# Local attention's routing and row projections move from the mixing piece into the global attention piece; all key sums first, values last

## The chip, the cores and the metric

The kernel runs on one core of one Trainium2 chip. What counts is the device time of one execution in microseconds (us), over all eight images. The engines are TensorE (PE, with its weight loads as PEld), VectorE (DVE), ScalarE (ACT), GpSimd (Pool) and SyncE (SP, which issues most DMAs).

## The reference, cut to what matters

Eight images of 128 channels and 32x32 points go through a local attention block with a convolutional tail, then a global attention block, then a mixture of experts.

```
# local attention ("a"): windows of 2x2 points, 256 windows, 4 selected by 8 heads x 16 channels
q, kv = rows(x) @ wq, rows(x) @ wkv            # per point
logit = mean(q) @ mean(k).T ; idx = top_k(logit, 4)      # routing
k_sel, v_sel = kv[idx]                          # 4 windows x 4 points = 16 keys
out = softmax(q . k_sel) . v_sel + dwconv5x5(v) # "lepe": 25 taps
x = x + out
x = x + fc2(relu(dwconv3x3(fc1(x))))
# global attention ("c"): 1024 tokens, 4 heads x 32 channels, distance mask
t = t + softmax(q k^T * mask) v @ Wo            # of layernorm(t)
# experts: 8, the best 2 of each token
t = t + sum_e combine[:, e] * (gelu(t' @ w1[e]) @ w2[e])   # t' = layernorm(t)
```

## The kernel before, in words

Each engine has its own program, written out by hand and held together by counting semaphores. Each runs its queue strictly in order. The loop over images is software-pipelined over three images: in turn n the kernel runs the global attention and the experts of image n, the convolution block and the q, k, v of image n+1 (`second`), and the local attention's front of image n+2 (`first`). A turn has two pieces, `attention` and `mixing`.

**Attention.** 32 units u (8 blocks of 128 queries by 4 heads). For each, PE computes 128x1024 scores (`("scores", u)`), DVE multiplies them by the distance band and finds the maximum (`scale_scores`, L1069), ACT takes the exponential (L734), PE transposes the result (`("turned", u)`, L540), ACT copies it out (L742), and PE multiplies it by the values one block later (`times_values`, L591). `projected` adds the output projection `wo` to the residual in two halves. Between units, at those in `WINDOW_STEPS_AT`, DVE runs one step each of the local attention of image n+1: tile 1's softmax and its value steps.

**Mixing.** PE follows `mixing_order()`: layer norm of image n (`centred`, `var`, `rstd`), router, the 3x3 convolution of image n+1 as matmuls with diagonal weights (`("dw", ...)`, L505), `start` and `combine` of the experts' result, then for eight experts `hidden` (L557, gelu on ACT) and `expert` (L560), which DVE adds up in `accumulate` (L1179, eight instructions per expert). Beside the experts come `fc2` of image n+1 (L514), its layer norm, and its q, k and v, which DVE finishes in `values` and `low(h)` (L1166).

**Local attention of image n+2.** `first_half` on DVE: `sums` of the four points of a window (L895), `choose` (max and index of the logits, L918 and L922), and eight `rows(t, p)`, each of which adds the bias to one projection of 128 windows (L905 for q, L906 for k and v). SP stores KV to a table in DRAM when all are done (`store_table`); Pool gathers the four chosen windows into KVSEL (`gathers`, L1299), multiplies keys by queries in 8 halves per tile (`key_product`, L1312), and DVE sums the products over channels (`sum_products`, L952). Each product lies in one of two halves of KV, so `key_product` i waits until sum i-2 is done. Then come per tile the softmax steps (`less_maximum` L962 and L963, ACT's `a_exp`, `sum_keys` L968) and four pairs of value steps (`multiply_values` L976, `attend` L983). After the last key sum Pool runs the 25 `taps` of the 5x5 convolution, each a product (L1325) and a sum into XLEPE (L1328). `window_residual` adds the attended rows to XLEPE in the next turn (L1021) and raises `x1_ready`, for which `fc1` waits.

In `second_half` the steps run in this order: key sums of tile 0, its softmax, its value steps woven with the key sums of tile 1, tile 1's softmax, its values. The first 26 (`EARLY_STEPS`) run in mixing between the experts' accumulations, the last ten in attention.

**PSUM.** Ring A has two banks of 512 columns (`psA`), ring B three of 1024 (`psB`). An entry's bank is its place in the emission order modulo the number of banks, and PE waits until the entry before it on that bank has been read out (`b_free`). Routing, rows and the values of the image use ring A; ring B has 115 entries in a turn, so the ring's last entry, k of head 3, and the first of the next turn, `("scores", 1)`, share a bank.

Where the routing stood in mixing:

```
PROJECTIONS_AFTER = {("centred", 1, 1): [(0, 0), (0, 1)], ("fc1", 0): [(0, 2), (0, 3)], ("var", 1, 1): [(1, 0), (1, 1)],
                     ("fc1", 1): [(1, 2)], ("rstd", 1, 1): [(1, 3)]}
```

Of the kernel before, what the change touches and what calls it, by code (L numbers as in the profile page):

```python
# [79 lines left out]
class Ring:  # L80

    def __init__(self, entries, slots):
        self.place, self.uses = {}, [0] * slots
        for i, name in enumerate(entries):
            s = i % slots
            self.place[name] = (s, self.uses[s])
            self.uses[s] += 1

    def slot(self, name):
        return self.place[name][0]

    def turn(self, name, n):
        s, k = self.place[name]
        return n * self.uses[s] + k + 1


class SharedRing(Ring):

    def __init__(self, first, middle, second, slots):
        super().__init__(first + middle + second, slots)
        self.first, self.middle = first, middle

    def turn(self, name, m):

        s, k = self.place[name]  # L110
        if name in self.middle:
            m = m + 1
        turn = m * self.uses[s] + k + 1
        if not (isinstance(m, int) and m == 0 and name in self.first):
            turn = turn - sum(self.place[other][0] == s for other in self.middle)
        if isinstance(m, int) and m == IMAGES:
            turn -= sum(self.place[other][0] == s for other in self.first)
        return turn


RING_A = SharedRing(["windows", "logits"] + [("qkv", t, p) for t in range(WTILES) for p in range(PX)] + [("v", 0), ("v", 1)],
                    [("pv", t) for t in range(TT)], [("attended", t) for t in range(WTILES)], 2)


class EarlyRing(Ring):

    def __init__(self, entries, early, slots):
        super().__init__(entries, slots)  # L130
        self.entries, self.early = entries, early

    def turn(self, name, n):
        s, k = self.place[name]
        on_slot = [other for other in self.early if self.place[other][0] == s]
        if name in self.early:
            if isinstance(n, int) and n == 0:
                return on_slot.index(name) + 1
            n = n - 1
# [1306 lines left out]
```

## Time and profile before

| what | value |
|---|---|
| median of 3 runs | 2264.81 us (2260.95 to 2265.35) |
| the profiled execution: its own time / its span | 2260.87 us / 2259.3 us |
| mean granted TensorE clock | 0.853 |
| busy: PE, DVE, Pool, ACT | 71%, 65%, 50%, 41% of the span |
| chain that ended last | PE 40%, DVE 23%, issue 16%, ACT 6%, Pool 5% |
| DVE waits for PE's expert results (L1179 for L560) | 310.6 us in all |
| Pool waits for the table store before its gathers | 250.0 us in all |

Times are from the start of the span. "Busy" is the time in which instructions of an engine run; the granted clock is the share of full speed (2.4 GHz) that PE was given. In a timeline a row gives start, duration, engine, line, operation, output and inputs, and the number of equal instructions merged into it; in brackets stands the idle time of the engine just before it, and what ended that. Rows below come from one turn of the loop, 849 to 1120 us, and a few from the start.

### The profile page before, as it was taken

The numbers are of one execution on the slowest core, as the hardware profiler recorded it, in microseconds if no ns is written. First come the engines' busy times: TensorE is split into PE (matmuls) and PEld (weight loads), VectorE is DVE, ScalarE is ACT, GpSimd is POOL, SyncE is SP. The second block draws the span as 40 slices with busy tenths as digits, with TensorE's granted clock in tenths as the row PEclk, the third lists the DMA queues.
The fourth block names the chain that finished last, engine by engine and source line by source line (L and its number), as shares of the span: only waits on it lengthen the run. The fifth ranks groups of instructions, "written<-read, shape, count | busy, mean of one in ns | idle before, by whom it ended". The sixth has DMA issues, their size and how long they took to land.

```text
span 2259.3 us, 39866 instructions
## 1 busy us (share of the span) xinstructions
PE 1611.4 (71%) x15168; PEld 1058.7 (47%) x15168; DVE 1471.6 (65%) x2564; ACT 933.5 (41%) x1285; POOL 1121.6 (50%) x582
## 2 busy tenths in 40 slices
PE   2004658895689857887578966788667875789897
PEld 1002325553455535555355544555355553555565
DVE  3893488638883498726886288854888268951654
ACT  0001237432563226633374234634256332754682
POOL 0994549433692329724495346934288233950000
PEclk9557878998799878988798987999779897989999
DMA  4201100030001100030000300011000200000000
GB/s 128 74 0 66 48 0 2 5 109 0 11 1 67 48 10 1 2 104 10 10 1 1 105 9 11 1 62 52 10 1 1 94 10 10 1 1 1 10 2 10
DMA packets 26138, 61.75 MB, mean 27 GB/s; under 512 B 4192, under 2 KB 13408, under 8 KB 25824
## 3 DMA queue, kind: packets, MB, share of 16 engines
q0 software_dynamic: 9216, 33.56, 4.3%
q1 hardware_dynamic: 16736, 25.60, 3.5%
q8 instruction: 131, 2.15, 0.4%
q14 instruction: 55, 0.45, 0.1%
HBM read 46.56 MB, written 12.58 MB: 26 GB/s over the span
## 4 chain that ended last, share of the span: by engine, by line
PE 40%; DVE 23%; issue 16%; ACT 6%; POOL 5%; DVEq 1%; ACTq 0%; POOLq 0%
PE psB L505 7%; PE psB L560 6%; DVE Q L983 6%; PE psB L540 5%; PE psB L408 5%; DVE P L1069 4%; DVE PT L1179 3%; PE psB L557 3%; POOL XLEPE L1328 3%; PE psB L514 3%; DVE STACKED L1166 2%; PE psA L591 2%; DVE KVSEL L952 2%; PE psA L423 2%; POOL KV L1325 2%
## 5 line engine op out<-in xcount | busy, mean ns | idle before, releaser
L1328 POOL TENSOR_TENSOR XLEPE<-XLEPE,KV 128x1024 f32<-128x1024 f32 x200 | 509.6, 2548 | 16.7
L1312 POOL TENSOR_TENSOR KV<-KVSEL,Q 128x1024 f32<-128x1024 f32 x112 | 267.4, 2406 | 444.9 <-DVE KVSEL L952 229.9
L540 PE MATMUL psB<-W,P 128*128 128x128 f32 x2048 | 319.6, 305 | 107.7 <-DVE NEGMAX L1069 100.7
L1069 DVE CUSTOM_DVE_ANT_0 P<-psB,W 128x1024 f32<-128x1024 f32 x256 | 312.3, 1220 | 99.8 <-PE psB L408 56.8
L734 ACT ACTIVATE P<-P,NEGMAX 128x1024 f32<-128x1024 f32 x256 | 293.0, 1145 | 186.4 <-DVE NEGMAX L1072 184.4
L1325 POOL TENSOR_SCALAR KV<-V_PAD,W 128x1024 f32<-128x1024 f32 x200 | 280.3, 1402 | 138.3 <-DVE KVSEL L952 98.3
L540 PEld LDWEIGHTS psB<-W,P 128*128 128x128 f32 x2048 | 257.4, 156 | 184.9 <-DVE NEGMAX L1069 96.4
L1179 DVE SCALAR_TENSOR_TENSOR PT<-psB,PT 128x128 f32<-128x128 f32 x512 | 138.2, 343 | 313.8 <-PE psB L560 310.6
L742 ACT ACTIVATE PT<-psB 128x1024 f32<-128x1024 f32 x256 | 260.7, 1018 | 59.4 <-PE psB L540 56.5
L408 PE MATMUL psB<-STACKED 96*128 96x512 f32 x512 | 205.9, 490 | 78.8 <-DVEq L1169 60.5
L560 PE MATMUL psB<-W,P 128*128 128x128 f32 x1024 | 159.6, 321 | 128.1 <-DVEq L1169 44.4
L983 DVE TENSOR_REDUCE Q<-PROD 128x128 f32<-128x2048 f32 x64 | 239.3, 3738 | 0.3
L560 PEld LDWEIGHTS psB<-W,P 128*128 128x128 f32 x1024 | 149.6, 231 | 160.5 <-issue 66.0
L1299 POOL DMA_INDIRECT KVSEL<-window_table,CHOSEN x64 | 60.9, 952 | 290.1 <-DMA window_table<-KV 250.0
L505 PE MATMUL psB<-H_PAD,DIAG 32*32 32x512 f32 x4608 | 167.9, 631 | 16.9 <-ACTq L687 14.8
L408 PE MATMUL psB<-TN,W 128*96 128x512 f32 x256 | 142.3, 707 | 45.8 <-DVEq L1169 45.8
L591 PE MATMUL psA<-PT,V 128*32 128x128 f32 x4096 | 170.2, 291 | 3.3 <-issue 2.2
L746 ACT ACTIVATE P<-psB,W 128x1024 f32<-128x1024 f32 x64 | 71.1, 1111 | 222.7 <-PE psB L557 222.7
L753 ACT ACTIVATE STACKED<-psB,W 96x1024 fp32r<-96x1024 f32 x64 | 70.2, 1108 | 207.4 <-PE psB L408 207.4
L591 PEld LDWEIGHTS psA<-PT,V 128*32 128x32 f32 x4096 | 103.6, 114 | 89.3 <-issue 88.5
L505 PEld LDWEIGHTS psB<-H_PAD,DIAG 32*32 32x32 f32 x4608 | 101.2, 105 | 84.1 <-issue 56.0
L408 PEld LDWEIGHTS psB<-STACKED 96*128 96x128 f32 x512 | 90.9, 218 | 93.8 <-DVEq L1169 65.6
(126 smaller groups left out, 2131.8 us busy)
## 6 DMA issues: line engine op xcount, KB each, us to landing
window_table<-KV SPq DMA_DIRECT2D x8, 1024.0 KB, 4.4
X<-x_by_window_dram SPq DMA_DIRECT2D x8, 512.0 KB
XLEPE<-x_dram SPq DMA_DIRECT2D x8, 512.0 KB, 3.5
out_dram<-PT SPq DMA_DIRECT2D x8, 512.0 KB, 3.4
W<-packed_dram SPq DMA_DIRECT2D x1, 3714.5 KB, 11.6
KVSEL<-window_table,CHOSEN POOLq DMA_INDIRECT x64, 5.4
FC<-packed_dram SPq DMA_DIRECT2D x8, 64.0 KB, 2.3
PROD<-gains_dram SPq DMA_DIRECT2D x1, 256.0 KB, 12.0
```

Of the source, the lines that this page charges most:

```text
L408: mm = pe.matmul(ps[:, h * HALF:(h + 1) * HALF], lhs, rhs[:, h * HALF:(h + 1) * HALF], **kw)
L505: mm = pe.matmul(banks[q][32 * j:32 * j + 32], DIAG[rows, TAPS3 * (2 * i + parity) + tap, :], H1_PAD[rows, parity, 16 * top + dy:16 * top ...
L540: mm = pe.transpose(ps[:, t * 128:(t + 1) * 128], P[:, i % P_BUFFERS, t * 128:(t + 1) * 128], ident)
L560: mm = pe.matmul(ps[:, t * 128:(t + 1) * 128], HG[:, i % 2, t * 128:(t + 1) * 128], w("w2", 128 * i, 128 * i + 128), **whole)
L591: pe.matmul(psA[s][rows, 0:128], V[:, t, rows], PT[:, (HEADS_C * c + h) % TURNED_BUFFERS, t, :], start=t == 0, stop=t == TT - 1)
L734: act.activation(P[:, b, :], P[:, b, :], ACT.Exp, bias=NEGMAX[:, b, 1:2], accum_out=L[:, q, h:h + 1]).then_inc(p_ready, 1)
L742: act.activation(PT[:, u % TURNED_BUFFERS].rearrange("k t q -> k (t q)"), psB[s][:], ACT.Copy).then_inc(b_free[s], 1)
L983: chain.mark(dve.tensor_reduce(Q[:, t, q, :], PROD[:].rearrange("p (k f) -> p f k", k=KEYS), AX.X, ALU.add))
L1069: dve.tensor_tensor_reduce(P[:, b, :], ps[:], w("band", at, at + TOK), 1.0, -3.0e38, ALU.mult, ALU.max, NEGMAX[:, b, 0:1]).then_inc(free, 1)
L1312: pool.tensor_tensor(PRODUCTS[i % 2].rearrange("p (k c) -> p k c", c=C), KVSEL[:, t, keys, 0:C], Q[:, t, q, :].unsqueeze(1).broadcast_to([ ...
L1325: pool.tensor_scalar(product, V_PAD[:, dy:dy + SIDE, dx:dx + SIDE], col("lepe_w", tap), 0.0, ALU.mult, ALU.add).then_inc(tap_ready, 1)
L1328: pool.tensor_tensor(acc, acc, product, ALU.add).then_inc(lepe_done, 1)
```

## The change

- Ring B takes the local attention's PE work: `windows`, `logits`, four `rows` (two projections at a time) and `image values`. The first six stand in the attention piece, behind units 1, 3, 6, 8, 10 and 12 (`ROUTED_AT`); `image values` stands in mixing, before `fc1`. Ring B then has 122 entries in a turn. Ring A keeps `pv` and `attended`.
- DVE's `sums` opens attention. `choose` and the four `rows(i)` (each two projections with one add for q and one for k and v) run behind `scale_scores(u)` for u = 5, 8, 10, 12, 14. ACT's `a_windows` runs in attention.
- Scratch moves: the attended rows, the window sums and the window queries and keys go to key columns of tile 1 in KVSEL, and the tap product to those of tile 0. So Pool's `gathers` now wait for `x1_ready` as well, and DVE's first `rows` no longer for all taps of the image before.
- DVE's steps of the local attention: 16 key sums, both `less_maximum`, both `sum_keys`, tile 0's values, tile 1's values. 28 run in mixing: two before the experts' choice, two within it, two after, then between the accumulations. Eight value steps of tile 1 stay in attention.
- ACT takes both `a_exp` in mixing, while its table for the exponential is loaded.

```diff
+        self.emitted = first + [(name, n + ahead(name)) for n in range(IMAGES) for name in body if n + ahead(name) < IMAGES]
...
+ROUTING = ["windows", "logits"] + [("rows", i) for i in range(WTILES * PX // 2)]
+ROUTED_AT = dict(zip((1, 3, 6, 8, 10, 12), ROUTING))
...
         if u + AHEAD < UNITS:
             order.append(("scores", u + AHEAD))
+        if u in ROUTED_AT:
+            order.append(ROUTED_AT[u])
...
-WINDOW_STEPS_AT = [3, 5, 8, 11, 14, 17, 19, 22, 25, 28]
+EARLY_STEPS = 28
+WINDOW_STEPS_AT = [4, 7, 11, 14, 17, 20, 23, 27]
...
+        ATTENDED = KVSEL[:, 1, 0:WTILES * PX, 0:C].rearrange("p (t q) c -> p t q c", t=WTILES)
+        X_SUM4, QWIN, KWIN = (KVSEL[:, 1, at:at + WTILES, 0:C] for at in (8, 10, 12))
+        TAP = KVSEL[:, 0, :, PX * HEADS_A:PX * HEADS_A + TOK // KEYS]
...
+                elif kind == "rows":
+                    t, first = divmod(2 * i, PX)
+                    for p in range(2):
+                        at = (first + p) * WINS + t * 128
+                        mm = pe.matmul(ps[:, p * HALF:p * HALF + 384], X[:, at:at + 128], w("wqkv"), **whole)
+                elif kind == "image values":
+                    mm = two_halves(ps, w("wqkv", 256, 384), X, **whole)
...
+                tiles = range(WTILES)
+                return ([step for t in tiles for step in key_steps(t)]
+                        + [lambda t=t: less_maximum(t) for t in tiles] + [lambda t=t: sum_keys(t) for t in tiles]
+                        + [step for t in tiles for step in value_steps(t)])
...
+                front = first_half(first) if first is not None else []
+                run(front, 1)
                 for u in range(1, UNITS):
                     scale_scores(u, n)
+                    if u - 2 in ROUTED_AT and u - 2 > 1:
+                        run(front, 1)
                     if u in WINDOW_STEPS_AT:
                         run(steps, 1)
...
+                run(steps, 2)
                 if n is not None:
-                    experts_chosen(n)
+                    experts_chosen(n, steps)
+                run(steps, 2)
                 accumulate(0, n)
-                run(steps, 2)
+                run(steps, 3)
                 if second is not None:
                     fc2_residual(second, chain)
+                run(steps, 3)
                 accumulate(1, n)
-                run(steps, 2)
+                run(steps, 3)
                 accumulate(2, n)
-                run(steps, 2)
+                run(steps, 3)
...
                         pool.wait_ge(pv_done, WTILES * m)
+                        pool.wait_ge(x1_ready, m)
```

## Rows read from the trace of the kernel before

**Rows 1.** Windows: window and length; PE, PEld, DVE, ACT, POOL busy; clock; DMA.

```profile
853.70:949.00 95.30, 76.07 (x829) 54.58 (x831) 81.98 (x130) 68.95 (x98) 88.65 (x47) 0.89 0.01 1
949.00:1119.80 170.80, 127.73 (x1079) 79.47 (x1069) 96.70 (x190) 48.11 (x64) 53.15 (x29) 0.84 0.12 41
...
1055.70:1119.80 64.10, 35.19 (x116) 20.94 (x115) 55.81 (x63) 13.51 (x14) 19.80 (x10) 0.77 0.03 9
```

**Rows 2.** Timeline of DVE in mixing.

```profile
961.23 0.76 DVE L918 MAX8 TOP<-psA 128x8 f32<-128x256 f32 x2 [1.89 <-PE psA L439]
...
963.74 0.41 DVE L906 TENSOR_TENSOR KV<-psA,W 128x256 f32<-128x256 f32 x1
...
978.90 0.23 DVE L1115 TENSOR_REDUCE PT<-psB 128x8 f32<-128x64 f32 x1 [0.24 <-DVE KV L906]
...
984.47 0.23 DVE L1143 TENSOR_TENSOR PT<-PT 128x64 f32<-128x64 f32 x1
1020.72 2.16 DVE L1179 SCALAR_TENSOR_TENSOR PT<-psB,PT 128x128 f32<-128x128 f32 x8 [36.02 <-PE psB L560]
...
1061.77 1.21 DVE L952 TENSOR_REDUCE KVSEL<-KV 128x64 f32<-128x1024 f32 x1
1062.90 3.63 DVE L983 TENSOR_REDUCE Q<-PROD 128x128 f32<-128x2048 f32 x1
```

**Rows 3.** Timeline of PE in mixing.

```profile
952.21 1.02 PE L529 MATMUL psB<-SQ,W 128*128 128x512 f32 x2
...
955.68 0.70 PE L432 MATMUL psA<-PROD,W 128*128 128x256 f32 x2 [2.01 <-DVEq L1025]
...
963.15 0.91 PE L423 MATMUL psA<-W,X 128*128 128x384 f32 x2 [1.43 <-DVEq L924]
...
965.62 1.45 PE L423 MATMUL psA<-W,X 128*128 128x384 f32 x4
...
969.07 2.07 PE L423 MATMUL psA<-W,X 128*128 128x384 f32 x4 [1.21 <-DVEq L908]
...
980.33 9.96 PE L505 MATMUL psB<-H_PAD,DIAG 32*32 32x512 f32 x288
...
995.54 1.04 PE L548 MATMUL psB<-W,PT 128*8 128x128 f32 x8
...
1059.00 3.60 PE L408 MATMUL psB<-TN,W 128*96 128x512 f32 x8
```

**Rows 4.** Timeline of POOL behind the taps: first gather, first two products.

```profile
984.45 0.99 POOL L1299 DMA_INDIRECT KVSEL<-window_table,CHOSEN  x1 [33.64 <-DMA window_table<-KV]
...
993.88 4.66 POOL L1312 TENSOR_TENSOR KV<-KVSEL,Q 128x1024 f32<-128x1024 f32 x2 [4.71 <-DMA KVSEL<-window_table,CHOSEN]
```

**Rows 5.** Lines by form, whole span: count, busy and mean ns, idle before.

```profile
L976 DVE TENSOR_TENSOR PROD<-KVSEL 128x2048 f32<-128x2048 f32 x32 | 98.7, 3085 | 0.1
...
L976 DVE TENSOR_TENSOR PROD<-KVSEL,S 128x2048 f32<-128x2048 f32 x32 | 78.3, 2446 | 5.5 <-DVE PT L1179 4.6 <-DVE STACKED L1166 0.5
```

**Rows 6.** Timeline of DVE from the last `low` through attention.

```profile
849.13 1.28 DVE L1166 SCALAR_TENSOR_TENSOR STACKED<-psB,W,STACKED 32x1024 fp32r<-32x1024 f32 x1 [0.33 <-DVE STACKED L1166]
853.76 1.23 DVE L1069 CUSTOM_DVE_ANT_0 P<-psB,W 128x1024 f32<-128x1024 f32 x1 [3.35 <-issue]
...
859.41 1.42 DVE L963 TENSOR_TENSOR KVSEL<-KVSEL,SUMS 128x512 f32<-128x512 f32 x1
...
889.50 4.26 DVE L976 TENSOR_TENSOR PROD<-KVSEL 128x2048 f32<-128x2048 f32 x1
...
893.77 1.19 DVE L1069 CUSTOM_DVE_ANT_0 P<-psB,W 128x1024 f32<-128x1024 f32 x1
...
922.48 1.23 DVE L1069 CUSTOM_DVE_ANT_0 P<-psB,W 128x1024 f32<-128x1024 f32 x1 [0.40 <-PE psB L408]
```

**Rows 7.** Timeline of PE in attention: the scores of one unit.

```profile
878.43 0.71 PE L408 MATMUL psB<-STACKED 96*128 96x512 f32 x2
```

**Rows 8.** Timeline of DVE before the loop: the residual of `fc2`.

```profile
255.46 1.65 DVE L1149 SCALAR_TENSOR_TENSOR XR<-psB,W,XLEPE 128x512 f32<-128x512 f32 x2 [24.12 <-PE psB L514]
```

More of the change, by code:

```diff
@@ L80 @@
 class Ring:
[L84 to L89, printed above, removed]
-    def slot(self, name):
[L92 to L106, printed above, removed]
-    def turn(self, name, m):
[L110 to L118, printed above, removed]
@@ L121, with __init__ @@
[L121 to L139, printed above, removed]
-        turn = n * self.uses[s] + k + 1 + len(on_slot)
-        if isinstance(n, int) and n == IMAGES - 1:
-            turn -= sum(self.entries.index(other) < self.entries.index(name) for other in on_slot)
-        return turn
+    def __init__(self, first, body, ahead, slots):
+        self.first, self.body, self.ahead = first, body, ahead
+        self.place = {name: i % slots for i, name in enumerate(body)}
+        self.emitted = first + [(name, n + ahead(name)) for n in range(IMAGES) for name in body if n + ahead(name) < IMAGES]
@@ new lines, in slot @@
+    def slot(self, name):
+        return self.place[name]
+    def turn(self, name, m):
+        s = self.place[name]
+        if isinstance(m, int):
+            before = self.emitted[:self.emitted.index((name, m)) + 1]
+            return sum(self.place[other] == s for other, _ in before)
+        on_slot = [other for other in self.body if self.place[other] == s]
+        first = sum(self.place[other] == s for other, _ in self.first)
+        return (m - self.ahead(name)) * len(on_slot) + first + on_slot.index(name) + 1
@@ L336, in x_is_free @@
             def x_is_free(m):
-                for h in range(2):
-                    sp.wait_ge(a_ready[RING_A.slot(("v", h))], RING_A.turn(("v", h), m - 1))
+                sp.wait_ge(b_ready[RING_B.slot("image values")], RING_B.turn("image values", m - 1))
                 sp.wait_ge(xsum_ready, m)
@@ L754, in high, with attention @@
                                    bias=col(f"b{kind}_c", h)[0:96]).then_inc(high_ready, 1)
-            def attention(n, second):
+            def attention(n, first):
                 exp(0, n)
@@ L764, in attention @@
                     turned(u, n)
-                    if second is not None and u == WINDOW_STEPS_AT[0]:
-                        a_exp(1, second)
+                    if first is not None and ROUTED_AT.get(u) == "windows":
+                        a_windows(first)
                     if u == PROJECTED + 3:
@@ L1104, in attention, with experts_chosen @@
                 normaliser(TT - 1, n)
-                assert not steps
-                if first is not None:
-                    first_half(first)[0]()
+                assert not steps and not front
                 attended(TT - 2, n)
                 attended(TT - 1, n)
-            def experts_chosen(n):
+            def experts_chosen(n, steps):
                 ps, free = arrived("router", n)
@@ L1187, in mixing @@
             def mixing(n, second, first, chain):
[L1188 removed]
+                steps = []
                 if first is not None:
[L1190 removed]
                     steps = second_half(first)[:EARLY_STEPS]
```

230 lines of the change are left out of this document (100 added, 130 removed).

## The prediction

> **What bounds the kernel now.** I read the windows of one full turn of the loop first, then VectorE's (DVE's) timeline, then who it waits for on TensorE (PE) and GpSimd (Pool). A turn takes 266.1 us: 95.3 of attention, 170.8 of the mixing piece. In attention DVE is busy 82.0 of 95.3 us and PE 76.1, so neither has much room; in the last 64 us of mixing DVE is busy 55.8 and PE 35.2 [rows 1]. Before that, DVE sits idle for 36.0 us, from the end of the experts' choice (984.7) until expert 0's matmuls end [rows 2]: there PE's queue is the bound. So a turn is three pieces in series: a PE piece up to expert 0, a DVE piece to the end of mixing, and attention, where DVE and PE alternate. I count mixing as x, us after 952.21, the start of the second `wo` product [rows 3].
>
> **1. Routing leaves the front of mixing.** PE loses there windows and logits (0.7+0.7 and 1.0, taken at the rates around them) and eight projections, 1.45 us for two, so 8.2 us [rows 3]. With them go the waits that DVE's routing steps cause PE: 2.0, 1.4 and 1.2 [rows 3]. The 3x3 convolution, now at x = 28.1, could start at 28.1 - 12.8 = 15.3. With nothing else, the `combine` transposes, now at x = 43.3, would come at about 31, that is 12.3 earlier.
>
> Something else is late next. The DVE now runs two key sums ahead of the experts' choice and two within it. Their products need the gathers, which now wait for `x1_ready`, since the attended rows lie in the key buffer: x = 4.7 (`projected` 0.7 from x = 1.1, then eight residual pieces, 2.4). From the first gather to the first product is 9.4 us, and one product takes 2.35 [rows 4]. Products 0 and 1 end at 16.5 and 18.9, Pool then issues four gathers (5.0), and products 2 and 3 end at 26.3 and 28.8. The fourth key sum ends at 30.1, and what is left of the choice, 4.9 of its 5.8 us (978.9 to 984.7) [rows 2], ends at x = 35.1. Now it ends at 32.5. ScalarE and the router's bank wait for its first half, at 21, earlier than anyone needs it; PE's `combine` waits for its second half. So `combine` starts at 35.1, not 31: **expert 0 comes 43.3 - 35.1 = 8.2 us earlier**. Bounds: 12.3 if the products are no hindrance; 4 if the gathers land 4 us later.
>
> **2. From expert 0 to the end of mixing.** Before, DVE needs 94.5 us from 1020.7 to about 1115.2. Only 6 of 16 key sums fit ahead of `accumulate(0)` (queue order), so 10 stay: 6 x 1.21 [rows 2] = 7.3 saved. Tile 1's softmax steps come in from attention (1.05, 0.75, 1.1, 0.35): +3.3. Then three things are added.
> (a) The taps start once all key sums are done, some 27 us after expert 0, so they lie beside the value multiplies of this piece. Multiplies of tile 0 take 2.45 us on average, those of tile 1, beside taps, 3.09, single ones 4.26 against 2.29 [rows 5, 6]. I take +1.0 for each of four and 0.7 for the softmax subtraction, 4.6 (bounds 0 and 8).
> The Trainium skill, "SBUF — State Buffer", "Who interferes with whom", says that a DVE instruction with two SBUF inputs contends with a GpSimd instruction that reads SBUF, and that the loser blocks fully. The 4.26 row agrees; if each multiply lost a whole tap instruction, this term would be 8 and not 4.6.
> (b) Nothing stands any more between `accumulate(4)`, `values` and `low(0)`. Head 0's q needs expert 4's bank, so it starts only when `accumulate(4)` ends; q and k take PE 3.6 us [rows 3], ScalarE's copy of 1.1 stands behind each, and expert 5 is queued behind them: 3.6 lost. At the end nothing lies between `accumulate(7)` and `low(3)` either: 3.0 lost.
> (c) From the sixth sum on a product can start only when the sum two before it has ended, so steps in threes wait 1.4 us for Pool, three times, one of them within the wait for `fc2`.
> Sum: -7.3 + 3.3 + 4.6 + 6.6 + 2.8 = 10.0. Against it go the waits of now that vanish: 5.3 before `accumulate(4)` (ScalarE waits for the first softmax there) and about 1.4 beside `fc2`. **+3.3 us.** Bounds: -5 (no new wait) and +8.
>
> **3. Attention.** Taken out: tile 1's softmax steps. Brought in: DVE's `choose` (max and index, 961.2 to about 963.2, so 2.0) and four double bias adds, each a 256-wide add (0.41) and a 512-wide one (between that and the 1.23 of a 1024-wide one, 0.7): 1.2 with settling [rows 2, 6]; PE's windows 1.4, logits 1.0, four row pairs 1.45 each. Moved work alone is +6.8 on DVE, -3.3 for the softmax steps.
> The order costs more. Ring B has three banks. Each of these entries comes after `scores(u+3)` and takes the bank of `scores(u+2)`; DVE runs it right behind `scale_scores(u+2)`. So PE can't start it before that ends, and DVE waits out the whole matmul, 1.45 + 0.2. And `scores(u+4)` then has the bank of `scores(u+3)`, so after the next scaling DVE waits for the 0.7 us of scores [rows 7] as well. Once in this trace such a place exists: behind `wo(0)` DVE waits 0.40 for the scores [rows 6].
> Walked through unit by unit from the end of `low(3)` (850.4 now): the X sum lies in the gap of 3.35 us before the first scaling [rows 6], since 122 entries, not 115, make `scores(1)` use q3's bank instead of k3's (-1.0). Then scaling 5 starts at 11.7, choice 14.3 to 16.2, scaling 8 at 23.8, rows 0 at 26.8, scaling 10 at 30.3, rows 1 at 34.8, multiply 37.5, scaling 12 at 40.4, rows 2 at 43.4, rows 3 at 51.4, reduction 52.6, scaling 15 at 56.4. Now scaling 15 starts at 893.8 - 850.4 = 43.4 [rows 6]: +13.0. But four value steps remain and not five (one reduction of 3.6, of which 2.8 counts, as PE catches up behind it), and the taps are over some 30 us into attention, 2.7: -5.5. **+7.5 us.** Bounds: 0 (all waits in slack: 6.8 - 3.3 - 3.5) and +14 (PE at the lower clock level behind each wait).
>
> **4. Free edits.** Scratch moved into KVSEL, SUMS per tile, QWIN and KWIN in two pieces: sizes don't change. The taps' product is now strided; if that made Pool slower, the taps would still have some 70 us, as they now end at 951 (984.5 less the 33.6 of Pool's wait) and would end near 885 [rows 4]. The table store leaves the chain: Pool's wait of 33.6 us for it [rows 4] becomes one for `x1_ready`. `load_x` goes out at x = 8 and is needed in attention.
>
> **5. Ends.** Before the loop, image 1's mixing has no experts. DVE waits 24.1 us for `fc2` [rows 8], and 7 key sums fit ahead of it instead of 2; the other 9 are paced by Pool (2.4), then both tiles' softmax steps stand ahead of `normalise` and so of v, q and k. Sums end at about 276, `normalise` at 283 (now 275), `low(3)` at 331 (now 325.3): +6 (0 to 10). Attention of image 6 has no routing, loses the softmax steps and the taps beside it: -7; one more wrap -1.
>
> **Sum.** A turn: -8.2 + 3.3 + 7.5 = +2.6; six turns +16; ends -2: +14 us on the profiled execution of 2260.9. The median of the runs is 2264.8, 0.2% above it; with the same +0.6% I forecast **2279 us**.
>
> **The rivals.**
> - *Faster: attention absorbs the routing.* If DVE's waits at rows and scores lie in time in which it waits anyway (13.3 us of 95 are idle [rows 1]), attention gains 1 to 2 us instead of 7.5, and the 8 us at the front stand: -8.2 + 3.3 + 1.5 = -3.4 a turn, and to -8 if the banks in mixing don't stall either. 6 x -5.5 - 2 = -35: 2230. For it: the model of the walk is serial and each term small. Against: 2.5 us already pass between the two scalings around `wo(0)`, and PE has 80% of attention full. It decides from attention below +5 us.
> - *Break-even*, within 4.5 us: the three terms cancel.
> - *Much slower: PE's clock.* Waits of 3 us in attention and 6 in mixing put PE on the lower level; the granted clock in the last 64 us of mixing is 0.77 against 0.89 in attention [rows 1]. Row pairs and scores at half speed add about 5 us a turn: +44, 2309.
> - *Pool holds the choice longer.* If products 2 and 3 come 4 us later, the front gives 4 and not 8: +38, 2303. For it: gathers of both tiles and `load_x` now share the DMA queues.
>
> **How the numbers follow.** Forecast (2267 to 2300) 0.43; faster rival 0.29; break-even 0.12; clock 0.10; Pool 0.06. A change of this kernel can be told from none above about 0.2%, 4.5 us. Slower 0.59, same 0.12, faster 0.29. Range 2236 to 2312: it reaches to the first rival's milder half and to the clock rival.
>
> **What would show it.** Expert 0's first accumulation some 8 us nearer to the second `wo`, with a wait of PE at `combine` for DVE; idle time of DVE before L1179 well under 36 us; DVE waits for the row matmuls of 1.5 to 3 us, four per image; multiplies above 3 us in mixing and 2.3 late in attention; attention 100 us and over. Wrong if attention stays within 3 us of now, or if `combine` waits for nobody.

## The result, and the profile after

| kernel | median of its runs (lowest to highest) | ratio to before, 95% interval |
|---|---|---|
| before, on the same chip | 2262.88 us (2259.03 to 2265.35) | |
| after | 2366.18 us (2361.84 to 2376.31) | 1.0464 [1.0427, 1.0502] |

The change makes the kernel 4.6% slower, 103 us; the forecast was 2279 us, within 2236 to 2312. The direction was right, the size was not: +14 us were forecast. The profiled execution of after is its slowest run, 2376.31 us, 10 us above its median.

First the windows of one steady turn of after, cut at the three places of the prediction. The turn begins at 1176.6, where the last `low` ends. The five windows are attention up to scaling 15 in two pieces (1176.6 to 1182, where only the head stands, and on to 1240), the rest of attention up to the second `wo` (1297.0), the front of mixing up to expert 0's first accumulation (1363.2), and the rest of mixing.

```profile
1176.60:1182.00 5.40, 2.50 (x10) 1.94 (x10) 2.05 (x2) 0.00 (x0) 5.03 (x4) 0.56 0.03 5
1182.00:1240.00 58.00, 38.50 (x314) 26.91 (x314) 39.68 (x66) 31.57 (x44) 27.27 (x15) 0.88 0.05 19
1240.00:1297.00 57.00, 49.13 (x608) 35.72 (x609) 39.98 (x76) 40.06 (x57) 0.00 (x0) 0.89 0.01 2
1297.00:1363.20 66.20, 54.90 (x711) 34.23 (x710) 20.57 (x60) 19.95 (x28) 26.34 (x16) 0.85 0.22 73
1363.20:1459.90 96.70, 61.30 (x256) 36.05 (x254) 80.81 (x109) 26.40 (x33) 84.00 (x41) 0.84 0.04 12
```

And the same cuts of before (850.4 to 1116.6; these windows are finer than those of [rows 1]).

```profile
850.40:952.20 101.80, 82.45 (x910) 60.26 (x911) 82.70 (x133) 70.34 (x100) 93.47 (x49) 0.88 0.01 1
952.20:1020.70 68.50, 60.69 (x735) 36.30 (x734) 17.19 (x76) 20.74 (x30) 12.27 (x10) 0.88 0.25 86
1020.70:1116.60 95.90, 60.72 (x254) 37.52 (x253) 78.80 (x111) 25.99 (x32) 36.17 (x16) 0.82 0.04 12
```

Attention went from 101.8 to 120.4 us (+18.6), the front of mixing from 68.5 to 66.2 (-2.3), the rest from 95.9 to 96.7 (+0.8): +17.1 in this turn. The turns of images 0 to 5 are 109.7 us longer together, the work before the first turn 4.2, the last two turns 1.5. Attention is the loss, and in it DVE is no busier: 81.7 us against 82.7, in a stretch 18.6 us longer. So it waits.

Whom for is in the timeline of DVE. From the end of the last `low` to the second wait for scores behind scaling 15 these are the rows with a wait of 1 us or more for another engine, the head, scaling 16 (1241.77), and two of the value steps between:

```profile
1175.32 1.28 DVE L1110 SCALAR_TENSOR_TENSOR STACKED<-psB,W,STACKED 32x1024 fp32r<-32x1024 f32 x1 [0.44 <-ACT STACKED L694]
1179.92 1.96 DVE L836 TENSOR_REDUCE KVSEL<-X 128x256 f32<-128x1024 f32 x1 [3.33 <-issue]
1181.91 1.23 DVE L1010 CUSTOM_DVE_ANT_0 P<-psB,W 128x1024 f32<-128x1024 f32 x1
...
1187.74 1.22 DVE L1010 CUSTOM_DVE_ANT_0 P<-psB,W 128x1024 f32<-128x1024 f32 x1 [1.47 <-PE psB L371]
...
1189.21 3.48 DVE L921 TENSOR_TENSOR PROD<-KVSEL 128x2048 f32<-128x2048 f32 x1
...
1195.17 0.76 DVE L863 MAX8 TOP<-psB 128x8 f32<-128x256 f32 x2 [1.15 <-PE psB L430]
...
1207.74 0.42 DVE L848 TENSOR_TENSOR Q<-psB,W 128x256 f32<-128x256 f32 x1 [1.54 <-PE psB L435]
...
1217.15 0.42 DVE L848 TENSOR_TENSOR Q<-psB,W 128x256 f32<-128x256 f32 x1 [4.37 <-PE psB L435]
...
1226.37 0.43 DVE L848 TENSOR_TENSOR Q<-psB,W 128x256 f32<-128x256 f32 x1 [1.73 <-PE psB L435]
...
1234.18 0.42 DVE L848 TENSOR_TENSOR Q<-psB,W 128x256 f32<-128x256 f32 x1 [2.78 <-PE psB L435]
...
1235.52 3.58 DVE L928 TENSOR_REDUCE KVSEL<-PROD 128x128 f32<-128x2048 f32 x1 [0.32 <-DVE KV L850]
...
1241.77 1.23 DVE L1010 CUSTOM_DVE_ANT_0 P<-psB,W 128x1024 f32<-128x1024 f32 x1 [0.75 <-PE psB L371]
...
1245.54 1.23 DVE L1010 CUSTOM_DVE_ANT_0 P<-psB,W 128x1024 f32<-128x1024 f32 x1 [2.34 <-PE psB L371]
```

The four row adds (L848) wait 10.4 us together; at the 1.65 us of one product and its settling it would be 6.6. The reason for the larger ones is on PE, whose queue holds the row product behind scores that themselves wait for DVE:

```profile
1206.07 1.56 PE L435 MATMUL psB<-W,X 128*128 128x384 f32 x4 [1.90 <-DVE NEGMAX L1010]
...
1210.44 0.73 PE L371 MATMUL psB<-STACKED 96*128 96x512 f32 x2 [1.93 <-DVE NEGMAX L1010]
...
1212.34 1.97 PE L487 MATMUL psB<-W,P 128*128 128x128 f32 x8
...
1215.56 1.56 PE L435 MATMUL psB<-W,X 128*128 128x384 f32 x4
...
1240.36 1.22 PE L371 MATMUL psB<-STACKED 96*128 96x512 f32 x2 [5.34 <-DVE NEGMAX L1010]
...
1242.52 1.97 PE L487 MATMUL psB<-W,P 128*128 128x128 f32 x8
```

DVE waits for the row product, PE then waits for DVE to free the bank, and DVE for those scores: each engine idles in turn. Behind the wait of 1.93 the eight transposes (L487) take 1.97 us, and behind that of 5.34 again. Three more groups of them between 1176 and 1250 take 1.60 to 1.97, the others 1.04 to 1.10. So row product 1 comes late as well. The granted clock is 0.50 from 1212.4 to 1214.3 and from 1240.4 to 1245.3, the lower of its two levels (1.2 GHz).

In the front of mixing, DVE from the key sums to expert 0 (x counts from 1297.0):

```profile
1314.87 1.22 DVE L897 TENSOR_REDUCE S<-KV 128x64 f32<-128x1024 f32 x1 [4.91 <-POOL KV L1253]
...
1326.79 1.22 DVE L897 TENSOR_REDUCE S<-KV 128x64 f32<-128x1024 f32 x1 [1.11 <-POOL KV L1253]
...
1328.40 3.07 DVE L1066 TENSOR_TENSOR PT<-PT 128x64 f32<-128x64 f32 x1
...
1363.21 2.16 DVE L1123 SCALAR_TENSOR_TENSOR PT<-psB,PT 128x128 f32<-128x128 f32 x8 [24.70 <-PE psB L507]
```

and PE around `combine` (L495):

```profile
1311.88 12.35 PE L452 MATMUL psB<-H_PAD,DIAG 32*32 32x512 f32 x288
...
1336.13 1.87 PE L495 MATMUL psB<-W,PT 128*8 128x128 f32 x8 [6.48 <-DVEq L1088]
```

The convolution starts at x = 14.9 (forecast 15.3), but `combine` waits 6.48 us for DVE and starts at x = 39.1, not 35.1, and behind the wait it takes 1.87 us where it took 1.04 [rows 3]. The DVE row above it tells most of the delay: a product of 128x64 that took 0.22 us on average before takes 3.07. Pool runs four key products without a gap there:

```profile
1322.06 9.33 POOL L1253 TENSOR_TENSOR KV<-KVSEL,Q 128x1024 f32<-128x1024 f32 x4
```

One of them ends at 1329.08 and the next at 1331.38, and DVE's small product lies from 1328.40 to 1331.47: it sits out the rest of the one and the whole of the other.

### The profile page after: what moved, and what is told of

The parts are those of the page before. It is cut to its first block, busy times and chain, and to the rows that moved or that the text cites. A ratio compares the mean times of both kernels' runs of the same rounds, so it can differ in the third digit from the quotient of the medians.

```text
span 2374.8 us, 39761 instructions
## 1 busy us (share of the span) xinstructions
PE 1640.0 (69%) x15168; PEld 1067.5 (45%) x15168; DVE 1498.8 (63%) x2500; ACT 940.0 (40%) x1285; POOL 1130.7 (48%) x582
## 4 chain that ended last, share of the span: by engine, by line
PE 35%; DVE 31%; issue 20%; POOL 7%; ACT 5%; DVEq 1%; SPq 1%; DMA 1%; POOLq 0%; ACTq 0%
PE psB L371 8%; PE psB L487 6%; DVE PROD L921 5%; POOL KV L1253 5%; DVE KVSEL L928 5%; PE psB L452 5%; DVE PT L1123 4%; DVE P L1010 4%; PE psA L538 4%; PE psB L507 3%; DVE STACKED L1110 2%; PE psB L435 2%; POOL KVSEL L1240 2%; PE psB L504 2%; ACT P L675 1%
## 5 line engine op out<-in xcount | busy, mean ns | idle before, releaser
L1271 POOL TENSOR_TENSOR XLEPE<-XLEPE,KVSEL 128x1024 f32<-128x1024 f32 x175 | 430.9, 2462 | 14.6
L1253 POOL TENSOR_TENSOR KV<-KVSEL,Q 128x1024 f32<-128x1024 f32 x112 | 262.1, 2369 | 234.1 <-DVE S L897 189.7
L487 PE MATMUL psB<-W,P 128*128 128x128 f32 x2048 | 317.8, 305 | 53.1 <-DVE NEGMAX L1010 33.6
L487 PEld LDWEIGHTS psB<-W,P 128*128 128x128 f32 x2048 | 258.7, 155 | 124.8 <-issue 86.1
L371 PE MATMUL psB<-STACKED 96*128 96x512 f32 x512 | 213.2, 502 | 131.9 <-DVE NEGMAX L1010 110.8
L1267 POOL TENSOR_SCALAR KVSEL<-V_PAD,W 128x1024 f32<-128x1024 f32 x175 | 255.3, 1459 | 54.1 <-POOL XLEPE L1271 34.6
L928 DVE TENSOR_REDUCE KVSEL<-PROD 128x128 f32<-128x2048 f32 x64 | 236.5, 3696 | 3.1 <-DVE KV L850 1.9
L507 PE MATMUL psB<-W,P 128*128 128x128 f32 x1024 | 149.9, 308 | 56.2 <-DVEq L1113 48.6
L452 PE MATMUL psB<-H_PAD,DIAG 32*32 32x512 f32 x4608 | 177.6, 668 | 15.7 <-ACTq L628 15.5
L694 ACT ACTIVATE STACKED<-psB,W 96x1024 fp32r<-96x1024 f32 x64 | 70.2, 1108 | 295.5 <-PE psB L371 295.5
L507 PEld LDWEIGHTS psB<-W,P 128*128 128x128 f32 x1024 | 143.0, 221 | 88.3 <-DVEq L1113 50.4
L452 PEld LDWEIGHTS psB<-H_PAD,DIAG 32*32 32x32 f32 x4608 | 109.6, 108 | 81.6 <-issue 57.0
## 6 DMA issues: line engine op xcount, KB each, us to landing
PROD<-gains_dram SPq DMA_DIRECT2D x1, 256.0 KB, 12.3
```

What stands on the lines that cost most here:

```text
L371: mm = pe.matmul(ps[:, h * HALF:(h + 1) * HALF], lhs, rhs[:, h * HALF:(h + 1) * HALF], **kw)
L452: mm = pe.matmul(banks[q][32 * j:32 * j + 32], DIAG[rows, TAPS3 * (2 * i + parity) + tap, :], H1_PAD[rows, parity, 16 * top + dy:16 * top ...
L487: mm = pe.transpose(ps[:, t * 128:(t + 1) * 128], P[:, i % P_BUFFERS, t * 128:(t + 1) * 128], ident)
L507: mm = pe.matmul(ps[:, t * 128:(t + 1) * 128], HG[:, i % 2, t * 128:(t + 1) * 128], w("w2", 128 * i, 128 * i + 128), **whole)
L928: chain.mark(dve.tensor_reduce(ATTENDED[:, t, q], PROD[:].rearrange("p (k f) -> p f k", k=KEYS), AX.X, ALU.add))
L1253: pool.tensor_tensor(PRODUCTS[i % 2].rearrange("p (k c) -> p k c", c=C), KVSEL[:, t, keys, 0:C], Q[:, t, q, :].unsqueeze(1).broadcast_to([ ...
```

## The experiments

All times below are medians (e4 and e6 have one run each); the ratio is to the kernel before on the same chip. The stages are those of one steady turn of each profiled execution: attention, front, rest.

| kernel | time, us | ratio, interval | attention | front | rest |
|---|---|---|---|---|---|
| before | 2262.88 | | 101.8 | 68.5 | 95.9 |
| after | 2366.18 | 1.0464 [1.0427, 1.0502] | 120.4 | 66.2 | 96.7 |
| e1 one unit later | 2293.03 | 1.0133 [1.0094, 1.0173] | 107.0 | 66.2 | 96.4 |
| e2 order alone | 2192.69 | 0.9688 [0.9638, 0.9739] | 97.1 | 68.5 | 90.5 |
| e3 choice first | 2296.56 | 1.016 [1.0101, 1.0219] | 120.4 | 55.9 | 96.8 |
| e4 rows twice | 2409.44, one run | | 124.5 | 66.5 | 96.4 |
| e5 both repaired | 2159.30 | 0.9558 [0.9517, 0.96] | 104.5 | 51.2 | 87.6 |
| e6 pair before only | 2312.24, one run | | 118.8 | 58.9 | 96.5 |
| e7 sums in a gap | 2172.70 | 0.9599 [0.9551, 0.9647] | 110.1 | 54.1 | 88.4 |
| e8 thirty early | 2191.46 | 0.9701 [0.9657, 0.9745] | 104.2 | 55.9 | 95.5 |
| e9 step off the pair | 2354.01 | 1.0388 [1.0349, 1.0427] | 116.8 | 64.7 | 97.7 |
| e10 repaired, step off 11 | 2146.56 | 0.9468 [0.9436, 0.95] | 104.0 | 51.2 | 87.7 |

The turns of one execution differ, and this is one of them: e5's is its shortest (243.3 us of 243.3 to 251.6), e2's and before's are their longest. The means of the turns of images 0 to 5, attention, front and rest, are 101.6, 67.1, 95.8 for before, 120.2, 65.6, 96.9 for after, 96.4, 67.0, 90.6 for e2, and 105.8, 53.4, 88.4 for e5.

**e1: same work, DVE's step one unit later.** Is it the work in attention, or the place in the two queues?

```diff
-                    if u - 2 in ROUTED_AT and u - 2 > 1:
+                    if u - 3 in ROUTED_AT and u - 3 > 1:
```

> The changed kernel with one thing moved: DVE runs the choice and the four double bias adds one unit later, behind scale_scores(u+3) instead of scale_scores(u+2). Same work, same banks. Theory of places (DVE waits out each row matmul and then the scores behind it, because both hang on the scaling just ended): the waits of 1.2, 1.5, 4.4, 1.7 and 2.8 us before the choice and the adds shrink to under 0.5 each and attention falls from 120.4 to about 110 us a turn, total about 2366 - 60 = 2306. Theory of work (attention has no room for 9 us more on DVE and 8 on PE, wherever it stands): attention stays within 3 us of 120, total 2350 or more.

73 us less than after; attention 120.4 to 107.0, front and rest within 0.3. Groups of lines over the whole span, first of after, then of e1 (after the bar: busy and mean ns, then idle time before the group and who ended it):

```profile
L848 DVE TENSOR_TENSOR Q<-psB,W 128x256 f32<-128x256 f32 x32 | 13.6, 425 | 66.2 <-PE psB L435 65.9 <-DVE CHOSEN L867 0.2
```

```profile
L848 DVE TENSOR_TENSOR Q<-psB,W 128x256 f32<-128x256 f32 x32 | 13.5, 423 | 12.3 <-PE psB L435 12.3
```

The waits for the row products shrink from 65.9 to 12.3 us. With one unit more between product and reader, most of the pair of waits is gone: 13.4 us a turn were the price of the place alone.

**e2: the order alone.** The kernel before, with all key sums first, values last and both exponentials in mixing; routing and rows stay where they were.

```diff
-EARLY_STEPS = 26
+EARLY_STEPS = 28
-WINDOW_STEPS_AT = [3, 5, 8, 11, 14, 17, 19, 22, 25, 28]
+WINDOW_STEPS_AT = [4, 7, 11, 14, 17, 20, 23, 27]
...
+                return ([step for t in tiles for step in key_steps(t)]
+                        + [lambda t=t: less_maximum(t) for t in tiles] + [lambda t=t: sum_keys(t) for t in tiles]
+                        + [step for t in tiles for step in value_steps(t)])
...
+                run(steps, 8)
                 accumulate(0, n)
```

> The kernel before with only the order of DVE's local steps changed: all key sums first (eight of them ahead of accumulate(0), then two between the accumulations), then both softmaxes, then the values; eight value steps in attention. Routing, rows, scratch and ring A stay as before. If the order is good in itself: attention loses 4 to 5 us (tile 1's softmax is gone), the piece from expert 0 to the end of mixing loses 2 to 6, a turn 6 to 10 us shorter, total about 2263 - 45 = 2218. If the taps beside the value multiplies and the stall between accumulate(4), values and low(0) eat it: within 10 us of 2263 or above.

3.1% faster than before: 4.7 us less in attention, 5.4 in the rest of mixing. This half of the change is a gain by itself. Against it, e1 has routing and rows in attention at a tolerable place and spends 107.0 there: the moved work costs 9.9 us, its bad place in after another 13.4.

**e3: the experts' choice first.** After, with no key sums ahead of or within the choice, six behind it.

```diff
 def experts_chosen(n, steps):
...
-                run(steps, 2)
...
-                run(steps, 2)
                 if n is not None:
                     experts_chosen(n, steps)
-                run(steps, 2)
+                run(steps, 6)
```

> The changed kernel with the four key sums that stand ahead of and within the experts' choice put behind it (six behind it). If these sums and Pool's products beside the choice delay combine: combine starts at about 28 us behind the second wo and not at 39, the first accumulation comes at 53 to 57 instead of 66.2, total about 2366 - 60 = 2306. If PE's own queue (convolution, hidden, start) is what ends last there: combine at 35 or later, total above 2345.

70 us less than after, and the first accumulation at 55.9, as expected. PE of e3 in the turn whose second `wo` starts at 1251.27:

```profile
1251.27 1.02 PE L476 MATMUL psB<-SQ,W 128*128 128x512 f32 x2
...
1283.69 1.04 PE L495 MATMUL psB<-W,PT 128*8 128x128 f32 x8
```

`combine` starts at x = 32.4 (28 was expected; the six turns have 29.3 to 32.4), waits for nobody and takes 1.04 us. The front is 10 to 13 us a turn shorter than after's and 10 to 17 (13.2 in the mean) shorter than before's. So the move does give the front what its own part had promised, 12.3, once no key sum holds the choice.

**e6: only the pair within the choice moved behind it.** The first two sums stay ahead of the choice.

```diff
 def experts_chosen(n, steps):
...
-                run(steps, 2)
...
                     experts_chosen(n, steps)
-                run(steps, 2)
+                run(steps, 4)
```

> The changed kernel with only the two key sums within the experts' choice moved behind it; the two ahead of it stay. It tells apart the two reasons for the late combine. If Pool's second pair of products is what held it (DVE waits for products 2 and 3, and its small two-input operation lies beside them): combine at 30 to 33 us behind the second wo, as with no sum ahead at all, and total about 2300. If the first pair's wait holds as much: combine at 35 or more, total about 2330.

The front is 58.9 us in this turn, 54.3 to 56.7 in the other five. Over the six turns it gains 54.7 of e3's 70.2 us, and `combine` starts at x = 31.2 to 32.4, as expected for Pool's second pair. So the pair within the choice was most of the fault, about 9 us a turn; the one before it costs the other 2.6. This is one execution, at 2312 where about 2300 was expected. Its DVE, where now no product of Pool runs beside the choice:

```profile
1274.38 1.22 DVE L897 TENSOR_REDUCE S<-KV 128x64 f32<-128x1024 f32 x1 [1.16 <-POOL KV L1252]
...
1276.95 0.23 DVE L1065 TENSOR_TENSOR PT<-PT 128x64 f32<-128x64 f32 x1
```

0.23 us against 3.07 for the same instruction: DVE lost 2.84 us, more than one of Pool's products (2.33). In all six turns of after with local attention it ends 0.1 us behind the end of the second product that it meets. In e3 it meets one, and ends 0.1 us behind that one:

```profile
1267.70 2.31 DVE L1065 TENSOR_TENSOR PT<-PT 128x64 f32<-128x64 f32 x1
```

```profile
1267.55 4.71 POOL L1251 TENSOR_TENSOR KV<-KVSEL,Q 128x1024 f32<-128x1024 f32 x2 [5.99 <-DMA KVSEL<-window_table,CHOSEN]
```

The first of these two products ends at 1269.92. There the loss costs nothing, since e3's `combine` doesn't wait for DVE. Why DVE gets in between two products in e3 and not in after is not shown. That the instruction is held up at all agrees with the Trainium skill, "SBUF — State Buffer", "Who interferes with whom", by which a DVE instruction with two SBUF inputs contends with a GpSimd instruction that reads SBUF; the prediction had charged that to the large multiplies alone.

**e4: every row product issued twice.** The second repeats the first, so the output is the same and PE has 1.5 us more at each of four places.

```diff
-                        mm = pe.matmul(ps[:, p * HALF:p * HALF + 384], X[:, at:at + 128], w("wqkv"), **whole)
+                        for again in range(2):
+                            mm = pe.matmul(ps[:, p * HALF:p * HALF + 384], X[:, at:at + 128], w("wqkv"), **whole)
```

> The changed kernel with each of the eight row matmuls issued twice (same result), so each of the four row entries costs PE 2.9 us and not 1.45. Theory of places: DVE waits out the whole matmul, so the wait before each add grows by 1.4 and attention by 5 to 6 us a turn, total about +35. If the row matmuls lie in time in which DVE and PE have slack: attention grows by under 2 us.

One run, 43 us above after's median and 33 above its profiled run. Attention grows by 4.1 us in this turn and by 3.8 in the mean (1.0 to 6.3) for 6 us of PE work, less than the 5 to 6 expected and more than the rival's 2: most of a row product's length is on the path, though PE is idle for more than that in this stretch.

**e5: both repaired.** e1's lag, e3's choice, and 12 key sums ahead of `accumulate(0)`, then steps in twos.

```diff
-                    if u - 2 in ROUTED_AT and u - 2 > 1:
+                    if u - 3 in ROUTED_AT and u - 3 > 1:
...
-                run(steps, 2)
...
-                run(steps, 2)
+                run(steps, 12)
                 accumulate(0, n)
-                run(steps, 3)
+                run(steps, 2)
```

> The changed kernel with both places mended and the steps of mixing laid out anew: choice and bias adds behind scale_scores(u+3); no key sum ahead of or within the experts' choice, twelve between it and accumulate(0), then two steps in each gap and two between accumulate(4) and values. If the two losses are separate and the routing's move is worth something in itself: attention 107 us as in the run with the adds one unit later, 54 us to the first accumulation as with the choice first, and 87 to 91 for the rest, since six more key sums lie ahead of expert 0: a turn of 248 to 252, total 2150 to 2190, below the order alone (2193). If what is won at the front is given back behind expert 0 (PE's banks): a turn of 257 or more, total above 2210.

4.4% faster than before and 1.3 points better than the order alone. The windows of one turn of e5 (attention, front, rest):

```profile
1065.40:1169.90 104.50, 85.09 (x933) 61.37 (x934) 80.98 (x143) 71.00 (x101) 28.06 (x15) 0.92 0.03 12
1169.90:1221.10 51.20, 46.37 (x711) 29.03 (x710) 27.49 (x67) 20.11 (x28) 37.98 (x21) 1.00 0.29 94
1221.10:1308.70 87.60, 62.76 (x256) 37.41 (x254) 73.80 (x103) 26.12 (x33) 75.84 (x39) 0.86 0.05 13
```

Against e2 the front of this turn is 17.3 us shorter and attention 7.4 longer. In the mean of the six turns these are 13.6 and 9.4, and the rest is 2.2 shorter: the move pays, by some 4 us a turn, and the new layout of the steps gives the rest. How much of it e2 would gain by a new layout of its own was not tried.

**e7: the window sums out of the head of attention.** In after and e5 the sums (L836, 1.96 us) stand at the head of attention, and scaling 1 ends 1.9 us later than before. e7 is e5 with them behind `scale_scores(3)`, `windows` and `logits` behind units 2 and 4, and the choice behind scaling 7.

```diff
-ROUTED_AT = dict(zip((1, 3, 6, 8, 10, 12), ROUTING))
+ROUTED_AT = dict(zip((2, 4, 6, 8, 10, 12), ROUTING))
...
-                run(front, 1)
...
-                    if u - 3 in ROUTED_AT and u - 3 > 1:
+                    if u == 3 or u - 3 in ROUTED_AT and u - 3 > 2:
```

> The both-repaired kernel with the window sums behind scale_scores(3) instead of at the head of attention, and windows and logits behind units 2 and 4. The trace of the changed kernel shows 3.3 us at the head of attention in which DVE waits for nothing the profile shows, with the sums behind them, so the first scaling comes 5.3 us behind low(3) and not 3.4. If the sums are exposed there and hidden in DVE's wait for scores at unit 4: 1.5 to 2 us less a turn, 9 to 12 in all. If the piece is bound by total work: no difference (within 4 us).

No gain: the interval overlaps e5's, the median is 13 us above. Scaling 1 ends 1.9 us earlier in this turn, and by scaling 5 that is gone (15.4 us from the last `low` here, 15.1 in e5), as the multiply ahead of it lies earlier beside the taps and takes 4.36 us instead of 2.72. By scaling 15 the turn is behind (54.8 here, 47.9 in e5). Part of that is a second change: the choice now stands behind unit 7 together with a value step, the reduction of 3.78 us, and scaling 8 starts at 27.8 where e5 has 25.4. So e7 doesn't price the sums at the head alone.

**e8: thirty early steps.** e5 with two of tile 1's value steps between `accumulate(7)` and `low(3)`, where PE's q and k leave DVE a gap.

```diff
-EARLY_STEPS = 28
-WINDOW_STEPS_AT = [4, 7, 11, 14, 17, 20, 23, 27]
+EARLY_STEPS = 30
+WINDOW_STEPS_AT = [7, 11, 17, 20, 23, 27]
...
+                run(steps, 2)
```

> The both-repaired kernel with two of tile 1's value steps moved from attention to the gap between accumulate(7) and low(3), where DVE waits for q and k of head 3. If DVE has slack there (about 3 us) and a value pair costs attention 5 us: 2 to 3 us less a turn, 10 to 18 in all. If attention is bound by PE at that point: a turn 2 to 3 us longer.

32 us worse than e5, outside what either side of the expectation gave. The slack was not there: in e5 DVE waits 0.70 us ahead of `low(3)`, not 3, and the pair takes 4.18 + 3.65 us at that place. So it costs 7.9 us in the rest of mixing (95.5 against 87.6). It relieves attention by 0.3 in this turn, by 0.1 to 5.5 in the others (2.2 in the mean): value steps in attention are mostly covered.

**e9 and e10: two things behind one unit.** After, unit 14 has both row adds 3 and a value step, the `attend` reduction of 3.6 us; e9 moves that step to unit 16, and the next one from unit 17 to 18. In e5, a row add and a value step both stand behind unit 11; e10 moves the step to unit 10.

```diff
-WINDOW_STEPS_AT = [4, 7, 11, 14, 17, 20, 23, 27]
+WINDOW_STEPS_AT = [4, 7, 11, 16, 18, 20, 23, 27]
```

```diff
-WINDOW_STEPS_AT = [4, 7, 11, 14, 17, 20, 23, 27]
+WINDOW_STEPS_AT = [4, 7, 10, 14, 17, 20, 23, 27]
```

(The first on after, the second on e5. The first expectation's "one place earlier" is a slip: the step goes later. Its "reduction of rows" is the `attend` reduction.)

> The kernel after the change, with one routing or projection step taken away from behind score unit 14, where the reduction of rows now stands together with the last of the value work, and put one place earlier; the work is the same. Theory 'two things behind one unit': the matmul engine's idle time of 5.3 us behind that unit goes in part, the stretch from scaling 15 to the attention's end falls from 58.0 us to 54 or 55, and the whole comes out 18 to 24 us below the kernel after the change, at about 2345. Rival 'the sum of the work': only what is done counts, and the time stays within 5 us of 2366.

> The kernel with both repairs (e5), with the step behind score unit 11 moved to unit 10, so that the row projection does not stand behind the same unit as a value step. Theory 'two things behind one unit': 0 to 1.5 us less in each turn, a total of 2150 to 2160. Rival 'the sum of the work': the same as e5 within 3 us. A total above 2168 would speak against both: the place before matters as well.

e9's median is 12 us below after's, by the ratios 17; its profiled execution is 22 us shorter. Attention is 3.6 us shorter in this turn, 2.8 to 5.8 in the six. The size is near that expected. By place, all of it lies before scaling 15 (62.5 to 59.1). But that cut now has the reduction on its other side: the stretch behind stays at 57.7 although it has that step of 3.75 us more. PE of e9 behind row product 3:

```profile
1223.93 1.56 PE L435 MATMUL psB<-W,X 128*128 128x384 f32 x4
...
1228.41 0.73 PE L371 MATMUL psB<-STACKED 96*128 96x512 f32 x2 [2.04 <-DVE NEGMAX L1010]
```

A wait of 2.04 instead of 5.34. e10 is 13 us below e5 by the medians and 20 by the ratios (their intervals do not overlap), and below the range that either theory gave, though the turn shown is only 0.4 us shorter; the others gain 0 to 5.4, while attention of image 6 loses 5.5. Why this one place gives that much was not traced, so e10 supports neither theory. It is the fastest kernel of the study, 5.3% below before.

## Why the prediction was wrong

In its own terms, a turn: front -8.2, rest +3.3, attention +7.5, in sum +2.6. Measured: -2.3, +0.8, +18.6, in sum +17.1. The ends were forecast at -2 and came to +5.7.

**Attention, the step that failed.** The mechanism was the right one and the term was too small by 11.1 us. The prediction put scaling 15 at 56.4 us from the last `low`; it starts at 62.5. The timeline accounts for it: the window sums were to lie in the head's gap of 3.35 us [rows 6], but the gap of 3.33 is there still and the sums stand behind it (1.96), and scaling 4 then waits 1.47 for its scores, so the multiply behind it starts 3.2 late; it takes 3.48 instead of 2.29, as the taps are not over (1.1); and row product 1 comes behind transposes at the lower clock, where DVE waits 4.37 for it (1.4 beyond the walk, which took PE at full speed there). Between those places the walk holds: the choice comes 4.3 us late against it, row adds 0 too, row adds 2 by 6.4, scaling 15 by 6.1. What the head's 3.2 us cost by themselves is not shown: e7 takes the sums away from there and gains nothing, but it puts the choice beside a value step.

Behind scaling 15 it forecast 52.9 us and there are 57.9; before had 58.4. The credit of 5.5 for one reduction fewer and taps that end early did not come. It does in e2 (54.0), which has the same value steps there, and in part in e1 (56.5), which has row add 3 there besides. Windows of that stretch, after first, then e2:

```profile
1239.10:1297.00 57.90, 49.13 (x608) 35.72 (x609) 40.88 (x78) 40.06 (x57) 0.00 (x0) 0.89 0.01 2
```

```profile
873.60:927.60 54.00, 44.23 (x590) 32.72 (x591) 42.74 (x78) 39.73 (x57) 0.00 (x0) 0.97 0.01 1
```

Unit by unit, the 3.9 us lie at two places. From scaling 15 to 17 after takes 6.4 us and e2 3.8; from scaling 18 to 23 it is 13.3 and 12.1; the rest is equal (3.6 from 17 to 18, 35.0 from 23 to the second `wo`). At the first place PE comes out of its wait of 5.34 on the lower clock: scores, values, transposes and scores take 1.22 + 1.08 + 1.97 + 1.20 us, in e2 0.71 + 0.65 + 1.09 + 0.71. That is 2.3 of the 2.6. So this part hangs on the collision behind unit 14. e9, which takes the collision away, fits: it has a step of 3.75 us more in the stretch and needs no more time.

The second place can be priced by two runs with the same steps there. PE and DVE between scaling 20 and 23, e5 first:

```profile
1132.28 1.97 PE L487 MATMUL psB<-W,P 128*128 128x128 f32 x8 [2.52 <-DVE NEGMAX L1010]
1133.90 1.20 PE L371 MATMUL psB<-STACKED 96*128 96x512 f32 x2
1135.29 1.22 DVE L1010 CUSTOM_DVE_ANT_0 P<-psB,W 128x1024 f32<-128x1024 f32 x1 [1.24 <-PE psB L371]
```

then e7:

```profile
1142.83 1.09 PE L487 MATMUL psB<-W,P 128*128 128x128 f32 x8 [2.51 <-DVE NEGMAX L1010]
1143.68 0.70 PE L371 MATMUL psB<-STACKED 96*128 96x512 f32 x2
1144.61 1.23 DVE L1010 CUSTOM_DVE_ANT_0 P<-psB,W 128x1024 f32<-128x1024 f32 x1
```

PE waits equally long in both. The granted clock behind the wait is 0.50 in e5 and 1.00 in e7, and scaling 18 to 23 takes 13.3 and 12.1 us: 1.2 us for the clock alone. After has e5's rows there. The mean clock of the stretch is no measure, though: after's turns of images 1 and 5 have 0.86 in it, the others 0.89, and all take 57.8 to 57.9 us. Here the lower clock cost time where DVE waited for PE, and none elsewhere.

Split by the runs: the order gives attention -4.7 (e2; forecast -3.3 - 5.5 = -8.8), the moved work costs +9.9 at a lag of three (e1 less e2), the lag of two +13.4 (after less e1). The prediction had 6.8 of work and, as what is left of its +13.0 to scaling 15 (13.0 - 6.8 + 3.3), 9.5 of coupling, 16.3 together, against 23.3. The upper bound of +14 was passed as well: it was made of PE's clock alone, and had the order's credit in full.

**Front of mixing.** Removal was priced rightly (convolution at x = 14.9 for 15.3; with the choice free, e3's `combine` comes 10.9 us earlier than before and its front is 12.6 shorter, for "12.3 if the products are no hindrance"). The hindrance was 4.0 us larger than forecast: 0.9 for the fourth sum (it ends at x = 31.0 for 30.1, as the first gather starts at x = 5.6 for 4.7), 2.85 for the 128x64 product held up by Pool, 0.2 left over. Another 1.9 went between `combine` and expert 0, 27.1 us for 25.2, where PE starts at the lower clock after its wait. 8.2 - 4.0 - 1.9 = 2.3. The step that failed is "what is left of the choice, 4.9": it was taken at the length it has with Pool idle.

**Rest of mixing.** +0.8 for +3.3. The multiplies average 3.24 us where the walk had 3.45:

```profile
L921 DVE TENSOR_TENSOR PROD<-KVSEL,S 128x2048 f32<-128x2048 f32 x32 | 103.5, 3236 | 5.6 <-DVE PT L1123 2.6 <-DVE TN L1000 2.0 <-DVE STACKED L1110 0.6
```

that is +0.8 each over [rows 5]. Of the two stalls for q and k (b), the first came as forecast: PE's q waits 5.71 us for expert 4's bank and DVE then 3.29, for 3.6. The second, ahead of `low(3)`, was put at 3.0 and is 0.70, and this is most of the 2.5 us by which the piece beat the forecast.

```profile
1409.74 5.15 PE L371 MATMUL psB<-TN,W 128*96 128x512 f32 x8 [5.71 <-DVEq L1127]
```

```profile
1414.36 1.28 DVE L1110 SCALAR_TENSOR_TENSOR STACKED<-psB,W,STACKED 32x1024 fp32r<-32x1024 f32 x1 [3.29 <-ACT STACKED L694]
```

```profile
1456.90 1.28 DVE L1110 SCALAR_TENSOR_TENSOR STACKED<-psB,W,STACKED 32x1024 fp32r<-32x1024 f32 x1 [0.70 <-ACT STACKED L694]
```

**Ends.** Before the loop +4.2 (forecast +6). Image 6's turn -3.0: its attention -5.6 (forecast -7), its front +3.1. Image 7's +4.5, of which 3.1 lie in its front too; nothing was forecast for these fronts, and they were not looked into. Turn 0 lost 24.3, more than the others.

**The rivals.** "Attention absorbs the routing" fell: it needed attention below +5. With e1's lag, e3's order of the choice and more sums ahead of expert 0 the kernel is faster after all, at 2159 (e5), by the front, the rest and the order, and not because attention absorbs the work: against e2 it still pays 9.4 us. "PE's clock" at +44 named a part of the truth: the lower clock stands behind the waits in both pieces, some 3.5 us a turn behind scaling 15. But e1, which removes the waits at the row adds, wins 13.4. "Pool holds the choice longer" was right in its 4 us, and for another reason than late gathers. What was not tried is the move without the new order, since the new scratch lies in key buffers that the old order still reads, and the order alone with e5's layout of the steps.

## What to carry to other kernels

Where two in-order engines share a ring of banks, count the lag between the entry and its reader: in this ring of three the same work cost 23 us a turn at a lag of two units and 10 at a lag of three. Price a step that is moved into such a loop by walking both queues, with what stands ahead of it on the producer, and look twice at two steps behind one unit: taking one away gave 3.6 us a turn in e9. In e10 it gave 0 to 5.4, with a loss at the end. A chain of small vector instructions that another engine waits for is worth keeping free of inserted work: two sums of 1.2 us within it, with the waits for their products, cost 7 to 10 us a turn. Look for a step's free room in the trace of the kernel that it goes into: e8 reckoned with a wait of 3 us that was 0.70.

## What the runs showed of the hardware that was not expected

- A DVE product of 128x64 took 3.07 us beside Pool's products and 0.23 without. Its end follows the end of a Pool product by 0.1 us, in five turns of e3 (1.43 to 2.38 us) that of the one it meets, in after that of the next: the loss goes by what is left of Pool's instructions, not by DVE's own size.
- The front of mixing has the same 711 matmul records in after, e3 and e5. PE was busy 54.9, 50.85 and 46.4 us with them, at a granted clock of 0.85, 0.91 and 1.00: e5's front is 15.0 us shorter than after's, and 8.5 of that is less busy time for the same work, once PE no longer waits for the choice. The two can't simply be subtracted: e1's front has 51.66 us of busy time at 0.87 and is as long as after's.
- The same wait of PE (2.5 us) was followed by matmuls at a granted clock of 0.50 in e5 and of 1.00 in e7, and cost DVE 1.24 us and nothing: the wait alone doesn't tell which.
- The 3.33 us ahead of the first instruction of a turn, which the trace puts down to issue, stand before whatever is first in DVE's queue, the window sums in after and a scaling in before and e7. All twelve traces have them (3.18 to 3.49 us) ahead of the turns of images 1 to 5, where the loop goes round, and none has them ahead of image 0, the first turn, or of images 6 and 7, which stand behind the loop (0.4 to 1.6 us, not put down to issue). Work put first in the queue stood behind them in every turn.
